# Signing the second layer's wide weights while the middle images run, and the set variances two products later

## The reference

```python
x = x + L0(_gn(x))   # attention block, see below
x = x + L1(_gn(x))   # scan along the columns, forward and back, PReLU
x = x + L2(_gn(x))   # attention block
x = x + L3(_gn(x))   # scan along the rows, forward and back, ReLU

def attention_block(x, w1, b1, w2, b2, w3, b3, alpha):
    e1 = relu(w1 @ xf + b1)            # 64 rows: the narrow branches
    e2 = relu(w2 @ xf + b2)
    assembly = relu(w3 @ xf + b3)      # 512 rows: the wide branch
    attn = softmax(e1^T e2)            # 256 x 256 for each image
    return alpha * (xf @ attn^T) + assembly
```

## Time and profile before

| what | value |
|---|---|
| median of 3 runs | 250.05 us (250.04 to 250.06) |
| the profiled execution, its own time | 250.12 us |
| its span (first to last instruction) | 248.3 us |
| outside the span | 250.12 - 248.3 = 1.8 us |
| TensorE busy in the span | 242.5 us (98%) |
| VectorE busy | 173.8 us (70%) |
| GpSimd busy | 107.9 us (43%) |
| ScalarE busy | 100.1 us (40%) |
| granted TensorE clock, mean | 0.999 |

### The profile page before, as it was taken

How to read it: one execution, slowest core, us unless ns; L and a number is a source line. 1 busy time by engine, 2 the same in 40 slices (tenths; PEclk the granted TensorE clock), 3 DMA queues, 4 the chain that set the end, 5 groups by cost and what they waited for, 6 DMA issues and landing times.

```text
span 248.3 us, 11081 instructions
## 1 busy us (share of the span) xinstructions
PE 242.5 (98%) x4482; PEld 215.1 (87%) x4484; DVE 173.8 (70%) x659; ACT 100.1 (40%) x237; POOL 107.9 (43%) x154
## 2 busy tenths in 40 slices
PE   8999999999999999999999999999999999999995
PEld 2678787877699999999997887877877999999995
DVE  2699576997767777777788865689776555555553
ACT  2046676423964344443445395943366000000000
POOL 0556903195357656677633434000243523333432
PEclk9999999999999999999999999999999999999999
DMA  6999200000000000000000000000000000012212
GB/s 198 405 375 424 82 1 0 0 3 0 0 8 0 0 0 0 0 0 0 0 4 0 0 0 4 0 0 0 3 1 0 5 0 0 0 42 69 79 63 85
DMA packets 5200, 11.49 MB, mean 46 GB/s; under 512 B 832, under 2 KB 3264, under 8 KB 4672
## 3 DMA queue, kind: packets, MB, share of 16 engines
q1 hardware_dynamic: 4752, 10.73, 11.6%
q10 hardware_dynamic: 432, 0.56, 0.7%
HBM read 9.19 MB, written 2.10 MB: 45 GB/s over the span
## 4 chain that ended last, share of the span: by engine, by line
PE 91%; DVE 3%; DMA 2%; POOL 1%; issue 1%; ACT 1%; SPq 0%; POOLq 0%; DVEq 0%
PE banks L634 45%; PE banks L459 11%; PE banks L424 10%; PE banks L483 10%; PE banks L436 6%; PE banks L444 2%; DMA gavg<-in_gavg 2%; PE banks L367 2%; PE banks L452 1%; POOL rstd L1296 1%; PE banks L603 1%; DVE dev L940 1%; PE banks L391 1%; PE banks L402 0%; DVE dev L937 0%
## 5 line engine op out<-in xcount | busy, mean ns | idle before, releaser
L634 PE MATMUL banks<-state,wc 128*64 128x64 f32 x3712 | 110.4, 223 | 0.4 <-DVE state L1162 0.3
L634 PEld LDWEIGHTS banks<-state,wc 128*64 128x64 f32 x3712 | 110.0, 138 | 0.6 <-issue 0.4
L1149 DVE SCALAR_TENSOR_TENSOR state<-banks,negb,inb 128x64 f32<-128x64 f32 x116 | 29.3, 281 | 24.2 <-PE banks L634 24.1
L1296 POOL TENSOR_TENSOR rstd<-gvar,mhalf 128x2 f32<-128x2 f32 (+3 forms) x13 | 15.8, 1223 | 58.6 <-DVE gvar L952 54.9
L1155 DVE SCALAR_TENSOR_TENSOR sloped<-banks,par,share 128x64 f32<-128x64 f32 x120 | 30.7, 281 | 13.6 <-PE banks L634 12.5
L424 PE MATMUL banks<-xn,w 128*128 128x256 f32 x128 | 31.1, 387 | 0.0
L459 PE MATMUL banks<-probT,xT 128*128 128x256 f32 x128 | 29.6, 380 | 0.0
L459 PEld LDWEIGHTS banks<-probT,xT 128*128 128x128 f32 x128 | 24.2, 190 | 3.1
L424 PEld LDWEIGHTS banks<-xn,w 128*128 128x128 f32 x128 | 23.3, 191 | 3.5 <-issue 1.0
L813 ACT COPY banks<-inb 128x256 f32 (+1 forms) x28 | 10.6, 377 | 30.4 <-DVE state L1165 28.0
L1373 POOL TENSOR_TENSOR share<-share,bent 128x256 f32<-128x256 f32 x29 | 17.8, 612 | 5.5 <-ACT share L814 3.1
(11 more groups left out here) (136 smaller groups left out, 318.4 us busy)
## 6 DMA issues: line engine op xcount, KB each, us to landing
w<-in_w SPq DMA_DIRECT2D x2, 1024.0 KB, 12.6
xT<-in_xT SPq DMA_DIRECT2D x4, 512.0 KB, 12.5
wc<-in_wc SPq DMA_DIRECT2D x2, 1024.0 KB, 17.5
result<-xh SPq DMA_DIRECT2D x15, 128.0 KB, 1.8
x<-in_x SPq DMA_DIRECT2D x3, 512.0 KB, 9.0
x<-in_x SPq DMA_DIRECT2D x1, 256.0 KB, 4.2
x<-in_x ACTq DMA_DIRECT2D x1, 256.0 KB, 4.4
w<-in_w ACTq DMA_DIRECT2D x1, 256.0 KB, 5.0
```

Of the source, the lines that this page charges most:

```text
L634: mm = nc.tensor.matmul(bank[K * h + m][c:c + TILE, 0:COLS], wc[l][:, k, m * P + c:m * P + c + TILE], inb[:, 0, k] if zeroth else state[:, ...
L1149: nc.vector.scalar_tensor_tensor(new_state(q, h, k), like_new(q, product(k, h)), negb[:, k:k + 1], like_new(q, inb[:, t, k]), ALU.max, ALU ...
L1296: nc.gpsimd.tensor_tensor(rstd[:, c:c + width], gvar[:, c:c + width], mhalf[:, c:c + width], ALU.pow).then_inc(s.rstd, 1)
```

## The change

Two edits. In `signed_weights` the wait for `x_done` is taken away, for narrow and wide weights alike; GpSimd then goes on with the wide weights and their sums as soon as it is through with the narrow ones and the weights have landed. In TensorE's `image`, for the first image of l = 2, `group_variances(2, 1)` moves from behind wide product 7 to behind wide product 9.

```diff
@@ tensor engine, image()
                     relu_products(5, 8)
-                    if first and l == 2:
-                        group_variances(l, 1)
                     relu_products(8, 9)
                     if last:
                         group_variances(l + 1, 0)
-                    relu_products(9, min(12, before_turns))
+                    relu_products(9, 10)
+                    if first and l == 2:
+                        group_variances(l, 1)
+                    relu_products(10, min(12, before_turns))
@@ gpsimd, signed_weights()
                     for k in range(K):
-
-                        pool.wait_ge(att[0].x_done, 1 if done is s_signed12 else K * (1 + k // 2) + 1)
                         nc.gpsimd.tensor_tensor(w[:, k], w[:, k], sign[:, 0:1].to_broadcast([P, w.shape[2]]), ALU.mult)\
                             .then_inc(done, 1)
```

## The result

The changed kernel takes 253.14 us (median of 5 runs, 252.99 to 253.53) against 250.06 us for the kernel before: ratio 1.0113, 95% interval 1.0097 to 1.0129. It is 3.1 us slower. The profiled execution took 253.04 us, its span is 251.2 us (248.3 before), and TensorE's mean granted clock is 1.00.

A forecast was written before the change was run, and what follows sets the result against it. TensorE's list, holding 91% of the chain of waits, was taken to bound the kernel. On the profiled 250.12 us, +4.37 - 1.08 - 0.1 = +3.2 gave 253.3, stated as 253.2 us for the median; range 251.0 to 254.8.

The forecast's parts named there:

- The gain in the last image: Last image of layer 0, score products to output products: with GpSimd idle it takes 8.62 instead of 9.70 us, gain 1.08.
- the twin in l = 2: Last image of layer 2, with like VectorE and TensorE lists and GpSimd idle: 8.62 us from score products to output products.
- The walk through the pair: Layer 0, up to image 2's score products: VectorE operations each wait for a GpSimd operation; cost 4.37 us, bounds 1.6 to 5.5.
- The open place: L1003, the residual sums beside GpSimd: no row showed whether they wait; taken to wait, else 2.8 us late instead of 4.37.
- the rival in which it doesn't (251.7): L1003 doesn't wait for GpSimd: +1.6 us in all, 251.7 us, or 250.5 with the port tie won; chance 0.16.
- the rival of 254.4: `add_fifth` (L1028) waits for GpSimd too and ends 5.5 us late: +4.3 us in all, 254.4 us; chance 0.10.
- the later wait decides: Image 2's score products: ScalarE's lateness behind `add_fifth` sets 43.9 us; TensorE's 2.6 us from the copy lie inside it.
- The slack ahead of L436: TensorE's `narrow_branches(2)` behind the copy L1011: below 0.2 us of slack before a late copy makes TensorE late.
- One term: Cost of the first edit in layer 0, up to image 2's score products: 4.37 us, bounds 1.6 to 5.5.
- the last step: From the end of `add_fifth` to image 2's score products: 3.05 us, as before, so 40.85 + 3.05 = 43.9 us.
- The second edit: First image of l = 2: L391 loses a 0.35 us wait, output products then wait for the copy; gain 0.1, bounds 0 to 0.35.
- Rival E: TensorE stands for 2.4 and 1.9 us and its clock falls to 1.2 GHz for a while: 256 us; chance 0.04.

The follow-up runs named there:

- the half-width kernel: Changed kernel with each wide signing and each weight sum of l = 2 split into two operations of half the width: 250.09 us, ratio 0.9996.
- the kernel with `add_fifth` first: Changed kernel with `add_fifth` ahead of the first two `shifted` inputs of image 2 instead of behind them: 251.35 to 253.28 us, ratio 1.0086.

## Why the prediction was right

**The gain in the last image.** Put at 1.08 from the twin in l = 2 and measured at 1.07. L988 and L941 are back at 0.17 and 0.18 us.

**The walk through the pair.** The forecast ends against the trace after: second scaling 32.8 (32.92), `shifted` 34.90 (35.01), residual sums 37.6 (37.60), copy 37.9 (37.93), `add_fifth` 40.85 (40.75), all GpSimd work 41.4 (41.29). The open place was L1003 (L1004 after), which no row of before showed beside GpSimd. It does wait: its two take 2.66 us, and the rival in which it doesn't (251.7) is out. This agrees with the rule in the Trainium skill, "SBUF — State Buffer", section "Who interferes with whom", that an instruction with two SBUF inputs contends with GpSimd's reads; L1029 with one kept its 0.68 us, as the rule says too, so the rival of 254.4 is out.

**Who waits.** TensorE stood 2.24 us ahead of L436 (forecast 2.4) and 1.46 us ahead of L444 (forecast 1.9). That the later wait decides was argued then, and is shown now: `add_fifth` sooner gives 1.4 us back with the copy no sooner. The slack ahead of L436, put below 0.2 us, can be read from the half-width kernel: its copy ended 0.36 us later than before (35.60 against 35.24) and moved L436 by 0.18 (35.66 against 35.48 in the timeline).

**The size.** One term was too large: the pair costs 3.97 us, not 4.37. 0.10 of it is that image 1 began 0.10 us later in this execution, which the walk, in absolute times, did not know, and 0.10 that `add_fifth` ended earlier. The rest is in the last step: I took 3.05 us from the end of `add_fifth` to the score products, and it was 43.60 - 40.75 = 2.85 us. ScalarE's work between the two takes 0.1 us less; that it had to wait before for TensorE's narrow branches, long done now, is the likely reason, but no row shows it. The rest is that the chain dates TensorE's start before a little later (39.53 us) than the timeline does (39.46).

**The second edit.** Gain 0.1 forecast, 0.15 measured alone and together, with the wait at the copy. The sum was +3.2; the spans of the two profiled executions differ by 2.9, the medians by 3.1. That the median came out within 0.1 us of 253.2 is in part luck: the stages that were forecast give 2.75.

**The clock.** Rival E had 0.04, and it is half true: the clock does fall after such a stop, in three of the five timed runs, and costs nothing that can be seen; the wait behind it is the likely reason. Its price of 256 us was too high in any case: in a kernel without that wait the price was 253.24 - 251.6 = 1.6 us.

## What to carry to other kernels

An engine that looks idle isn't free room: ask what its operation locks, and lay the other engine's list beside it. Here long GpSimd operations belong where VectorE reads PSUM or takes batch statistics, and where they can't be moved they should be cut short, since a waiting operation pays for the rest of the one that runs (0.8 us against 4.0 for the same elements). When a wait is taken away, read what it had kept apart.

## What the runs showed of the hardware

A GpSimd power does not lock VectorE out, long as it is. In the changed kernel the power runs from 60.24 to 62.62 us, and the `shifted` inputs and residual sums inside it keep their times (0.34 and 0.44 us each, GpSimd and VectorE in that order):

```profile
60.24 2.38 POOL L1297 TENSOR_TENSOR rstd<-gvar,mhalf 128x12 f32<-128x12 f32 x1 [18.96 <-DVE gvar L953]
```

```profile
60.09 1.37 DVE L977 TENSOR_SCALAR shifted<-x,shift,sign 128x256 f32<-128x256 f32 x4
61.37 0.89 DVE L1004 SCALAR_TENSOR_TENSOR rx<-rel,sign,shifted 128x256 f32<-128x256 f32 x2
```

Its 12 elements in a partition take 2.38 us, powers of 2 elements 0.74 us, and L1302, GpSimd's next operation with the same shape, 0.21 us. So the lock for a whole instruction, which the prediction worked with, isn't held by every GpSimd operation, and most of that time goes into the power itself; that this is why the port is free is my reading, not a measurement. And one stop of TensorE of 2.3 us is enough for the clock to fall in some executions and not in others of the same program: in the kernel with `add_fifth` first the mean granted clock was 0.992 or 0.993 in three runs and 1.000 in two.
